# Second attention: one kind in eight of the row maxima taken over half the columns, as max(b + relu(a - b))

## The reference, cut to what matters

```python
q = (x @ Wq + bq).reshape(B, S, H, Dh)      # B 16, S 512, H 16, Dh 8
latent = x @ Wl + bl
k = (latent @ Wk + bk).reshape(B, S, H, Dh)
v = (latent @ Wv + bv).reshape(B, S, H, Dh)
scores = jnp.einsum('bihd,bjhd->bhij', q, k) * SCALE
attn = jax.nn.softmax(scores, axis=-1)
out = jnp.einsum('bhij,bjhd->bihd', attn, v).reshape(B, S, D)
out = out @ Wo + bo
```

## Time and profile before

| | |
|---|---|
| three runs | 4495.58, 4496.21, 4492.27 us (median 4495.58) |
| profiled execution | 4488.49 us, of which the span of instructions 4486.7 us |
| second attention, first to last row maximum | 2277.5 to 2998 us of the span |
| in 2400 to 2900 us of it | PE busy 494.5, DVE 472.0, ACT 411.1, POOL 236.5 of 500 us, granted clock 1.00 |

### The profile page before, as it was taken

One profiled execution on the slowest core, in us unless ns is written; L12 is line 12 of the kernel. 1 busy time (PEld: TensorE's weight loads), 2 busy tenths in 40 slices (PEclk: granted clock), 3 DMA queues, 4 the chain that ended last, 5 costly groups with the idle time before them and its releaser, 6 DMA issues. The chain is left out here.

```text
span 4486.7 us, 91792 instructions
## 1 busy us (share of the span) xinstructions
PE 3969.0 (88%) x30019; PEld 2002.6 (45%) x30020; DVE 3190.9 (71%) x7556; ACT 2844.3 (63%) x5771; POOL 2366.9 (53%) x2903
## 2 busy tenths in 40 slices
PE   7699999899688989889889999997988699996997
PEld 4244444463233333337323333336974244443896
DVE  3588888547899999984479999972126788886013
ACT  7488888767565555547758888873324477775332
POOL 3366666311599999970413444544545246556452
PEclk8799999999899999999979999998989799998997
DMA  9533333104533333310543333325665544442665
GB/s 276 176 90 87 87 88 87 28 0 160 187 131 133 119 126 134 132 64 0 183 148 90 88 89 90 92 68 168 213 207 180 165 112 110 117 113 79 205 213 197
DMA packets 515891, 564.61 MB, mean 126 GB/s; under 512 B 162498, under 2 KB 435523, under 8 KB 507280
## 3 DMA queue, kind: packets, MB, share of 16 engines
q1 hardware_dynamic: 497312, 521.88, 37.9%
q0 software_dynamic: 18160, 37.42, 2.3%
HBM read 399.39 MB, written 159.68 MB: 125 GB/s over the span
## 5 line engine op out<-in xcount | busy, mean ns | idle before, releaser
L1668 ACT ACTIVATE p_probs<-p_t_ps 128x512 f32<-128x512 f32 (+1 forms) x2048 | 1029.4, 557 | 336.2 <-PE p_t_ps L1427 144.9
L1448 PE MATMUL p_o_ps<-p_probs,p_v_st 128*32 128x256 f32 (+3 forms) x9728 | 748.9, 381 | 10.0 <-ACT p_o_sb L1630 9.4
L1761 DVE TENSOR_REDUCE p_row_max<-p_s_ps 128x1 f32<-128x512 f32 x1024 | 632.4, 677 | 51.1 <-PE p_s_ps L1376 51.0
L1376 PE MATMUL p_s_ps<-p_s_k,p_s_q 48*128 48x512 bf16 (+3 forms) x3072 | 607.9, 334 | 52.3 <-DVE p_row_max L1758 36.9
L2492 POOL TENSOR_TENSOR xn<-p_dtx,p_b_sb 128x512 f32<-128x512 f32 x512 | 633.5, 1271 | 34.4 <-DMA p_b_sb<-mamba_rows 17.4
L2564 DVE TENSOR_TENSOR_SCAN p_state<-p_da,xn 128x1024 f32<-128x1024 f32 x256 | 578.8, 2276 | 9.7 <-ACT p_da L2430 7.8
L1409 PE MATMUL p_t_ps<-p_t_q,p_t_k 50*128 50x512 bf16 (+3 forms) x3072 | 546.4, 333 | 36.3 <-ACT p_probs L1668 10.5
L2430 ACT ACTIVATE p_da<-p_dt,p_rate 128x512 f32<-128x512 f32 (+1 forms) x512 | 331.9, 679 | 279.5 <-DVE p_state L2564 277.8
L1758 DVE CUSTOM_DVE_ANT_0 p_tried<-p_s_ps,c_mask_row 128x512 bf16<-128x512 f32 (+3 forms) x1024 | 441.0, 485 | 79.6 <-PE p_s_ps L1376 72.7
L1758 DVE CUSTOM_DVE_ANT_0 p_tried<-p_s_ps,p_s_bias 128x512 bf16<-128x512 f32 (+3 forms) x1024 | 441.4, 481 | 76.0 <-PE p_s_ps L1376 74.4
L1312 POOL TENSOR_TENSOR p_probs<-p_probs,xn 128x384 f32<-128x384 f32 (+1 forms) x384 | 409.1, 1096 | 148.7 <-ACT p_probs L1666 148.3
(11 more groups left out here) (318 smaller groups left out, 7018.9 us busy)
## 6 DMA issues: line engine op xcount, KB each, us to landing
p_wb<-in_w SPq DMA_DIRECT2D x142, 512.0 KB, 3.5
p_b_sb<-mamba_rows SPq DMA_DIRECT2D x64, 1024.0 KB
p_s_q<-stack_q SPq DMA_DIRECT2D x384, 96.0 KB, 2.3
p_s_k<-stack_k SPq DMA_DIRECT2D x384, 96.0 KB, 2.4
p_t_q<-stack_q SPq DMA_DIRECT2D x384, 96.0 KB
p_t_k<-stack_k SPq DMA_DIRECT2D x384, 96.0 KB
p_raw<-routed_rows SPq DMA_DIRECT2D x142, 130.0 KB, 3.2
stack_q<-p_parts SPq DMA_DIRECT2D x48, 384.0 KB, 2.6
```

The lines of the kernel that those rows point to most:

```text
L1376: mm = pe.matmul(s_ps[:, slot, at:at + width], s_q[rows, g % 2, pair, c * P:(c + 1) * P], s_k[rows, g % 2, pair, 0:width], start=True, sto ...
L1448: mm = pe.matmul(o_ps[32 * j:32 * j + 32, at:to], v_st[:, g % 2, c, j, :], probs[:, g % 2, j, place[c] + at - first:place[c] + to - first] ...
L1668: act.activation(exps, tile, ACT.Exp, scale=scale).then_inc(expd, 1)
L1761: read = dve.tensor_reduce(found, scores, X, ALU.max)
```

## The change

For piece (pair 0, i 1), `FOLDED`, both r, in the second attention alone, the 512 keys are folded to 256 before the maximum. With `a` the scores of the first 256 keys and `b` those of the last 256, max(a, b) = b + relu(a - b):

- TensorE makes `b` in the first half of the bank, and in the second half `a` and then, on top of it, q times the negated keys: a - b. Three 256-wide matmuls stand where one 512-wide stood, and a wait for the negated keys.
- ScalarE writes relu(a - b) into `above` (`bend`), from PSUM to SBUF, 128x256. `bend` stands just behind the exponential of the same piece.
- VectorE waits for it (`bent`) and does an add of `b` and `above` with a running maximum, 128x256, in place of the 128x512 reduction.
- GpSimd negates the last 256 keys of each step into `k_less` (`turn_k`, 128x256, bf16), once a step, behind the copy of the values; it waits for the load of that step's keys. At the start it also clears the part of `s_k` which this reads, and SyncE's first loads wait for that.

```diff
@@ -1124,6 +1124,12 @@
         BY_DVE, BY_POOL, LATE = {(1, 0)}, {(0, 0), (0, 1), (1, 1)}, (1, 1)
         EXP_ORDER = [(1, 1), (0, 2), (0, 0), (0, 1), (1, 0), (1, 2)]
 
+    FOLDED = None if causal else (0, 1)
+    HALF_T = T // 2
+
+    def s_no(group, pair, i, r):
+        return USES_OF_GROUP * group + 2 * NTILE * pair + 2 * i + r + 1
+
     def exp_no(group, pair, i, r):
         later = 1 if (pair, i) == LATE else 0
@@ -1152,6 +1158,10 @@
         o_cat = ph.sb("o_cat", [P, T])
         tried = ph.sb("tried", [P, RING, T], BF16)
         s_seen = ph.sem("s_seen")
+        k_emptied, k_turned, bent = ph.sem("k_emptied"), ph.sem("k_turned"), ph.sem("bent")
+        if FOLDED:
+            k_less = w["room"][:, 0:HALF_T].bitcast(BF16).rearrange("p (u t) -> p u t", u=2)
+            above = w["room"][:, HALF_T:HALF_T + T].rearrange("p (r t) -> p r t", r=2)
         t_ps, s_ps = ph.ps("t_ps", [P, RING, T]), ph.ps("s_ps", [P, RING, T])
         o_ps, misc = ph.ps("o_ps", [P, T]), ph.ps("misc", [P, T])
@@ -1245,6 +1255,8 @@
                 sp.dma_start(shift_dram[ds(bb, 1), 4 * g:4 * g + 4].rearrange("a h c r t -> (a h c) r t"),
                              shift[:, g % 2]).then_inc(m_stored[g % 2], 16)
 
+            if FOLDED:
+                sp.wait_ge(k_emptied, 1)
             load_s(0, 0)
             load_s(0, 1)
@@ -1286,6 +1298,8 @@
         @block.gpsimd
         def _(pool):
 
+            if FOLDED:
+                pool.memset(s_k[:, :, FOLDED[0], HALF_T:T], 0.0).then_inc(k_emptied, 1)
             pool.memset(t_k[:, :, :, :], 1.0).then_inc(zeroed, 1)
             pool.memset(v_st[:, :, :, :, :], 0.0).then_inc(zeroed, 1)
@@ -1302,6 +1316,15 @@
                 at = 2 * DK * (g % 2)
                 pool.tensor_copy(v_st[:, g % 2, :, :, at:at + DK], v_raw[:, g % 2]).then_inc(v_ready, 1)
 
+            def turn_k(n):
+                if not FOLDED or n >= GROUPS:
+                    return
+                pool.wait_ge(s_loaded[n % 2], 64 * (n // 2) + 64)
+                if n >= 2:
+                    pool.wait_ge(s_mm, USES_OF_GROUP * (n - 1))
+                pool.tensor_scalar(k_less[:, n % 2], s_k[:, n % 2, FOLDED[0], HALF_T:T], -1.0, None, ALU.mult
+                                   ).then_inc(k_turned, 1)
+
             def add_bias(b, g, pair, i):
 
@@ -1333,22 +1356,28 @@
                     pool.wait_ge(misc_mm, read + 1)
                 pool.tensor_copy(rt.staged_x[:, :], x[:, T * m:T * m + T]).then_inc(rt.x_staged, 1)
 
+            for n in range(AHEAD + 1):
+                turn_k(n)
             rt.empty_rows(pool)
             for b in range(NB):
                 values(b, 0)
+                turn_k(4 * b + AHEAD + 1)
...
@@ -1372,6 +1401,15 @@
                 pe.wait_ge(s_read, USES_OF_GROUP * (4 * bb + g) + 2 * NTILE * pair + 2 * i + r + 1)
                 slot = bank(v + k // 4, g, pair, i, r)
                 rows = slice(HALF * r, HALF * r + ROWS)
+                if (pair, i) == FOLDED:
+                    pe.wait_ge(k_turned, 4 * bb + g + 1)
+                    q_of = s_q[rows, g % 2, pair, i * P:(i + 1) * P]
+                    k_of = s_k[rows, g % 2, pair]
+                    pe.matmul(s_ps[:, slot, 0:HALF_T], q_of, k_of[:, HALF_T:T], start=True, stop=True)
+                    pe.matmul(s_ps[:, slot, HALF_T:T], q_of, k_of[:, 0:HALF_T], start=True, stop=False)
+                    pe.matmul(s_ps[:, slot, HALF_T:T], q_of, k_less[rows, g % 2], start=False, stop=True
+                              ).then_inc(s_mm, 1)
+                    return
                 for at, width, c in s_tiles[i]:
                     mm = pe.matmul(s_ps[:, slot, at:at + width], s_q[rows, g % 2, pair, c * P:(c + 1) * P],
@@ -1632,6 +1670,17 @@
             if BY_POOL:
                 act.sem_inc(expd, 2)
 
+            def bend(group, v, r):
+
+                act.wait_ge(s_mm, s_no(group, *FOLDED, r))
+                if group:
+                    act.wait_ge(s_read, RING + s_no(group - 1, *FOLDED, r))
+                act.activation(above[:, r], s_ps[:, bank(v, group % 4, *FOLDED, r), HALF_T:T], ACT.Relu).then_inc(bent, 1)
+
+            for group in range(AHEAD if FOLDED else 0):
+                for r in range(2):
+                    bend(group, 0, r)
+
             def exp_added(group, pair, i):
 
@@ -1666,6 +1715,8 @@
                         act.activation(exps, tile, ACT.Copy).then_inc(t_copied, 1)
                     elif (pair, i) not in BY_DVE:
                         act.activation(exps, tile, ACT.Exp, scale=scale).then_inc(expd, 1)
+                    if (pair, i) == FOLDED and exists(b, g + AHEAD):
+                        bend(4 * b + g + AHEAD, v + (g + AHEAD) // 4, r)
                     if BY_POOL and r == 1:
                         if (pair, i) == (0, 1) and started >= 1:
@@ -1752,7 +1803,11 @@
                         slot = bank(v + k // 4, g, pair, i, r)
                         scores = s_ps[:, slot, at:at + width]
                         found = row_max[:, g % 2, r, pair, c:c + 1]
-                        if causal:
+                        if (pair, i) == FOLDED:
+                            dve.wait_ge(bent, 2 * (4 * bb + g) + r + 1)
+                            read = dve.tensor_tensor_reduce(tried[:, slot, 0:HALF_T], s_ps[:, slot, 0:HALF_T], above[:, r],
+                                                            1.0, LOWEST, ALU.add, ALU.max, found)
+                        elif causal:
                             over = (w["mask_row"][:, T - width:T] if bias is None
                                     else bias["s"][:, 4 * g + 2 * pair + r, T - width:T])
@@ -2690,7 +2745,8 @@
                         norm_w, wq=small["mla_w"][:, 0], wl=lw[:, :], bl=small["latent_b"][0:32, 0:1],
                         wk=small["latent_kv"][:, 0], wv=small["latent_kv"][:, 1],
                         bq=mb[:, 0:1], bk=mb[:, 1:2], bv=bv[:, :]))
-                attend(core, x, stacks, v_dram, shift_dram, dict(masks, wo=small["mla_w"][:, 1], bo=mb[:, 2:3]),
+                attend(core, x, stacks, v_dram, shift_dram, dict(masks, wo=small["mla_w"][:, 1], bo=mb[:, 2:3],
+                                                                      room=xn[:, NTOK // 2 + T:NTOK // 2 + 3 * T]),
                        DK ** -0.5, causal=False, routed=routing(True))
             elif name == "attn_b1":
                 with core.phase() as ph:
```

More of the change, by code:

```diff
@@ L1342, in _ @@
                 values(b, 1)
+                turn_k(4 * b + 1 + AHEAD + 1)
                 if b >= 3:
@@ L1348, in _ @@
                 values(b, 2)
+                turn_k(4 * b + 2 + AHEAD + 1)
                 if b >= 2:
@@ L1351, in _ @@
                 values(b, 3)
+                turn_k(4 * b + 3 + AHEAD + 1)
                 if b >= 1:
```

## The result

| | before | after |
|---|---|---|
| median of 5 runs each, same chip | 4492.99 us (4489.15 to 4496.21) | 4522.45 us (4515.67 to 4529.9) |
| ratio, 95% interval | | 1.0064 [1.0052, 1.0076] |
| profiled execution, its span | 4488.49, 4486.7 us | 4521.96, 4520.2 us |

The change makes the kernel 29.5 us slower (23 to 34 us by the interval). Forecast were 20.1 us more and a median of 4515.7 us; the measured 4522.45 us lie in the range of 4495 to 4535. The median of before rests on five executions. The three groups of 20 to 30 executions of before that were run with the experiments, on chips that need not be that of the table, have medians of 4494.86 to 4495.45 us, and against those the change costs 27.0 to 27.6 us.

What follows compares the result with a forecast made beforehand. Three engines were nearly full; the path ran from the read of piece 0 through TensorE to the reduction of piece 4. Steps 20.6 - 1.0 at the beginning + 0.45 memset = +20.1 us, giving 4515.7 us; range 4495 to 4535.

Steps and rivals of the forecast that it cites:

- beginning (up to step 0): First two steps' maxima: 4 shorter pieces save 1.0 us; SyncE's first loads wait 0.45 us for a memset.
- The saving falls into idle time: VectorE, pieces 2 and 3: 0.26 us less per piece, 33 us in all, goes into the idle time ahead of piece 4.
- ScalarE's order sets piece 4: Relus behind their exponentials make piece 4's reduction late by 0.25, 0.73 and 0.32 us in steps 28, 29 and 31.
- e: Start of ScalarE's exponential of piece 2, from which the distance to the reduction of piece 4 is counted.
- The sum of 2.20 us: Exponential of piece 2 to reduction of piece 4: two exponentials, two relus, hand-over 0.03, second half-width pass, `shift_high`.
- The third matmul: TensorE, piece 3: 256 more columns cost 0.10 us, deciding only where VectorE is not later already, as in step 30.
- ScalarE is not on the path elsewhere: ScalarE's added relus delay no later piece, since it is busy 37.36 of 45.44 us in a batch.
- GpSimd's cover: GpSimd's waits for keys and negations add 17.5 us to 21.6 of 45.4 a batch; counted as nothing.
- VectorE paces: Rival: VectorE's saving is had, 0.52 us a step, 32 us, 4463 us with the beginning; chance 0.09.
- The saving covers the wait: Rival: the relu's delay is made up, only TensorE's 0.10 us a step remains, 6 us, 4501 us; chance 0.16.
- ScalarE too is on the path: Rival: relus also delay exponentials of pieces 3 to 7, 33 us, 4539 us; chance 0.17 together with upper prices.
- GpSimd late: Rival: GpSimd's round outgrows the batch, 3 us a batch, 45 us, 4541 us; chance 0.02.

Runs made afterwards that it cites:

- e5: Kernel before, with the reductions of pieces 2 and 3 in the second attention over 256 of 512 columns only; 4495.03 us, ratio 1.0000.
- e6: Kernel before, with the reductions of pieces 6 and 7 over the first 256 columns only; 4484.65 us, ratio 0.9974.
- e4: Changed kernel without the relus and with VectorE's full 512-column reduction; three matmuls and GpSimd's negation stay; 4502.98 us, ratio 1.0016.
- e3: Kernel before, plus a 256-column ScalarE relu that nothing waits for, ahead of the exponentials of pieces 2 and 3; 4503.94 us, ratio 1.0018.
- e2: Changed kernel with both relus ahead of the exponential of piece 2; 4508.87 us, ratio 1.0029.
- e7: Changed kernel with the same work but no ScalarE-to-VectorE wait: relu reads key-major scores ahead of the exponential, VectorE adds a constant; 4507.35 us, ratio 1.0029.
- e8: Kernel before, with shift_low moved ahead of piece 4 in the second attention, right behind shift_high; 4488.57 us, ratio 0.9984.
- e10: Kernel before, with shift_low ahead of piece 4 and TensorE's turn of the output moved behind pieces 8 and 9; 4484.61 us, ratio 0.9977.
- e1: Changed kernel with each relu ahead of the exponential of its own piece, not behind it; 4507.73 us, ratio 1.0027.

## Why the prediction was right, and where its sizes were off

The mechanism was the one forecast, and the median lay 6.7 us above the 4515.7 of the sum. Where the 27.3 us of the phase came from, beside the 20.1 of the sum:

| | forecast | measured |
|---|---|---|
| beginning (up to step 0) | -0.55 | +0.4 |
| steps 0 to 7 | +1.46 | +2.1 |
| steps 8 to 59 | +18.2 | +23.4 |
| steps 60 to 62, to the start of the last | +0.98 | +1.4 |

**The saving falls into idle time.** Right. e5 shows it as exactly nothing, 0.00 us in each of the four steps, and e6 shows that it is the place and not the amount: four pieces later the same cut saves 0.6 us a batch.

**ScalarE's order sets piece 4.** Right, and the working carries over: from the exponential of piece 2 to the reduction of piece 4 there are now 2.32, 2.33, 2.40 and 2.36 us in steps 28 to 31, where it was 1.95, 1.47, 2.29 and 1.88. The differences, 0.37, 0.86, 0.11 and 0.48, are within 0.03 the growth of the steps, 0.36, 0.84, 0.11 and 0.45. All four steps hand on what piece 4 is late, as forecast. In the profile the signs came as named: the relu of piece 3 ends 1.63 us after e (1.6), VectorE's idle time is 1.17 and 0.33 us (1.1 and 0.4), the wait for TensorE ahead of piece 4 is gone, the step with g = 1 grows most. VectorE's busy time fell by 25 us, where some 30 were named: each pass now stands behind a wait and counts with its length and the read of its result, 0.43 us together, where the forecast had the 0.34 from start to start.

**The sum of 2.20 us was short by 0.13.** This is the term that was mis-sized, and it makes up nearly all of the 5.2 us by which steps 8 to 59 were too low: steps with g = 0, 1 and 3 grew by 0.11, 0.11 and 0.13 more than forecast, 13 times, 4.6 us. The hand-over was put at 0.03, read from a plain reduction behind a matmul. Here it is 0.14 to 0.15 from the end of the relu to the pass (2643.60 to 2643.74, 2644.35 to 2644.50). The relu to its end took 0.42 instead of 0.38, another 0.04, and the pass 0.35 instead of 0.34. Against these, the two exponentials took 0.48 and 0.47 instead of 0.49 each and the first relu 0.26 instead of 0.27: 0.12 + 0.04 + 0.01 - 0.04 = 0.13.

What makes the hand-over longer can be seen in VectorE's list. The plain reduction carries its wait itself. The pass of the change has two waits, for its scores and for the relu, and the one for the relu is an instruction of its own ahead of the pass (DVEq is VectorE's sequencer; the timeline leaves such rows out):

```profile
L1807 DVEq EVENT_SEMAPHORE  x128: 21/21/21, 2284.6 to 3022.5; - x128
```

In step 29 this instruction starts at 2643.635, 0.04 behind the relu's end, which is the hand-over of the forecast; the pass starts 0.11 behind it, at 2643.741. In the 124 cases of a wait for ScalarE the medians are 0.037 and 0.105. So the forecast had the step to the waiting instruction right and left out the step from there to the pass. The trace of before already showed it, since the passes of the third attention have such an instruction too (L1750). VectorE and TensorE there:

```profile
3818.26 0.39 PE L1376 MATMUL p_s_ps<-p_s_k,p_s_q 48*128 48x512 bf16 x2
...
3818.83 0.69 DVE L1758 CUSTOM_DVE_ANT_0 p_tried<-p_s_ps,c_mask_row 128x512 bf16<-128x512 f32 x1 [0.22 <-PE p_s_ps L1376]
```

The matmul ends at 3818.65, the wait's instruction starts 0.03 later, and the add and maximum 0.18 later. The distance should have been read from a row of the same instruction with a wait like its own. How much of it belongs to the separate wait and how much to this kind of pass stays open: no run has the pass carry the last wait itself. The prediction had 0.15 as the upper bound of the hand-over, and took its value from the wrong neighbour.

**The third matmul** was counted in step g = 2 alone, and that agrees with after (0.11 there). For a kernel without the late relu the argument would have been wrong: e4 shows that it costs 0.11 us in all four steps, because the path from the read of piece 0 through TensorE to piece 4 is tight in each of them. Here it was hidden behind the later relu.

**ScalarE is not on the path elsewhere** was argued from its busy time in the batch, "2 us a step to spare". An average was the wrong view. e3 finds it on the path in the step with g = 1, for 0.48 us a batch. It didn't falsify the sum only because the relu's lateness, 0.84 in the same step, covers it. Any repair of the order uncovers it, and this made the expectations of e2 and e7 some 6 us too low.

The Trainium skill, "ScalarE: Activation LUTs", section "Rules for kernel authors", puts relu on VectorE, and the runs don't contradict it for this place: ScalarE's work alone costs 0.48 us a batch (e3), its order in after 0.95 more than the work (after against e7). The 0.51 us for 256 columns, an estimate from the budget in that section, was too high: 0.416 was measured. The section gives its 0.3 us for an activation whose bias is a pointer operand, a condition that the prediction left out; the relu's row shows no such operand.

**Beginning and GpSimd.** +0.4 instead of -0.55. In the trace of after TensorE waits 0.44 us for the first negated keys, and the memset (0.52 us) stands in front of the loads. That this is what ate the saving is not shown: from the first memset to step 0 it takes 23.96 us in before and 24.37 in after, but 23.68 to 24.51 in e3, e8 and e10, which have no fold and leave the beginning all but as it was. After its first wait TensorE never waits for the negated keys. GpSimd's cover held: its batch has 24.95 us of work instead of 21.60.

**The rivals.** *VectorE paces* is refuted by e5. *The saving covers the wait* is refuted by the steps of after, and comes nearer for e1 and e2 (+12 and +13 us against its 6). *ScalarE too is on the path* exists, at one step in four and covered. *GpSimd late* did not come.

## What to carry to other kernels

Before paying for an engine's work with another's, ask at which instruction the two streams next meet, and whether the relieved engine already waits there: then the saving is worth nothing, however full the engine is, and moving a short piece of existing work into that wait (`shift_low`, e8) is the better use of it. Look for the next meeting point as well: in e8 and e10 what was won ahead of piece 4 was partly lost at the turn of the output. Ask the donor engine's slack step by step, not as an average over a batch. On an in-order engine the place of a new producer can cost more than its work: 0.95 us a batch for the order here, 0.48 for the work, and none of the 0.95 with the relu one instruction earlier. Read each hand-over from a row of the very instruction that will wait, and look whether its wait is an instruction of its own.

## What the runs showed of the hardware

How soon VectorE starts after a wait depends on where the wait stands. An instruction that carries the wait itself starts 0.03 to 0.04 us after the end of what it waited for: plain reductions behind a matmul 0.031 (90 cases in the trace of before), two-operand operations (TENSOR_TENSOR) behind ScalarE 0.032 (139 cases), medians of the waits over 0.15 us. With a wait as an instruction of its own ahead, the same kind of TENSOR_TENSOR starts 0.102 after it (60 cases), the add with running maximum 0.186 after a matmul (233 cases, 227 of them 0.17 to 0.19) and 0.142 behind ScalarE's relu in after (124 cases). In all three of these the wait's instruction itself starts 0.036 to 0.038 after the end. Where the wait is already met it costs nothing that is seen: the second pass of step 29 in e2 has such an instruction ahead and starts 0.34 us behind the first, like the second pass of the earlier trace rows, which has none.

A relu of 128x256 from PSUM between exponentials takes 416 ns but only 0.26 us from its start to the next instruction's.
